# First transfers cut in smaller pieces, products of zeros ahead of the first data, and a new place for the tokens' turn, in a two-layer gated cross-attention kernel

## The reference

```python
x = x + tanh(g_xattn[0]) * xattn0(layernorm(x), ctx)   # 16 heads of 16, softmax over 361 rows, then 256-512-256
x = x + tanh(g_ffn[0])   * moe0(layernorm(x))          # best one of 8 experts, 256-1024-256
x = x + tanh(g_xattn[1]) * xattn1(layernorm(x), ctx)   # ternary weights, 8-bit activations, two attentions
x = x + tanh(g_ffn[1])   * moe1(layernorm(x))          # 16 mixed projections to q, k, v, attention, 16 back

# inside xattn0, the part that the change touches
q = (x @ Wq + bq)      # from the normalised tokens
k = (y @ Wk + bk)      # from the context, 8 x 361 x 256
v = (y @ Wv + bv)
```

## Time and profile before

| | us |
|---|---|
| median of 3 runs | 621.48 |
| lowest and highest of them | 619.89, 621.88 |
| the profiled execution, its own time | 621.23 |
| its span from first to last instruction | 619.4 |
| PE busy | 594.3 (96% of the span) |
| DVE, ACT, POOL busy | 322.6, 217.9, 72.4 |

### The profile page before, as it was taken

One profiled execution on the slowest core, in us unless ns is written; L12 is line 12 of the kernel. 1 busy time (PEld: TensorE's weight loads), 2 busy tenths in 40 slices (PEclk: granted clock), 3 DMA queues, 4 the chain that ended last, 5 costly groups with the idle time before them and its releaser, 6 DMA issues.

```text
span 619.4 us, 9464 instructions
## 1 busy us (share of the span) xinstructions
PE 594.3 (96%) x3699; PEld 397.3 (64%) x3699; DVE 322.6 (52%) x762; ACT 217.9 (35%) x509; POOL 72.4 (12%) x69
## 2 busy tenths in 40 slices
PE   5989999999999989999999889999999999999996
PEld 4756444444556758999999658777565555555653
DVE  3695767588774751222222789885562233231452
ACT  2644565645673364112221565673200010001000
POOL 0043101000004401232221000000100100000000
PEclk9999999989999978999999999999999999999999
DMA  8910000100001562899995100700723832320000
GB/s 195 318 68 2 17 2 1 35 3 2 2 1 26 194 206 72 304 341 344 361 341 206 62 2 0 239 2 3 261 77 103 313 103 77 103 76 1 0 26 26
DMA packets 25195, 69.93 MB, mean 113 GB/s; under 512 B 5143, under 2 KB 12919, under 8 KB 21319
## 3 DMA queue, kind: packets, MB, share of 16 engines
q1 hardware_dynamic: 21798, 58.16, 28.5%
q0 software_dynamic: 3360, 11.28, 5.3%
HBM read 64.62 MB, written 4.80 MB: 112 GB/s over the span
## 4 chain that ended last, share of the span: by engine, by line
PE 83%; DVE 8%; ACT 4%; DMA 2%; issue 1%; POOL 1%; SPq 0%; DVEq 0%; ACTq 0%; POOLq 0%
PE bank L2048 21%; PE bank L1565 12%; PE bank L1884 8%; PE bank L1897 8%; PE bank L1712 7%; PE bank L2084 7%; PE bank L1686 5%; PE bank L1730 3%; PE bank L1655 2%; ACT region L1459 2%; PE bank L1718 2%; DVE nmax L1007 1%; PE bank L1546 1%; DVE stage L1018 1%; PE bank L2002 1%
## 5 line engine op out<-in xcount | busy, mean ns | idle before, releaser
L2048 PE MATMUL bank<-region,kvT 128*128 128x400 f32 x384 | 130.4, 500 | 0.0
L2048 PEld LDWEIGHTS bank<-region,kvT 128*128 128x128 f32 x384 | 72.4, 190 | 54.2 <-issue 0.3
L1147 DVE TENSOR_TENSOR region<-xT,stage 128x800 f32<-128x800 f32 x30 | 29.7, 992 | 69.7 <-PE bank L2048 69.5
L718 DVE TENSOR_REDUCE nmax<-bank 100x2 f32<-100x722 f32 x64 | 55.2, 905 | 15.7 <-PE bank L1686 15.3
L1884 PEld LDWEIGHTS bank<-stage,region 128*128 128x128 f32 x448 | 52.2, 192 | 1.4 <-issue 0.8
L1884 PE MATMUL bank<-stage,region 128*128 128x128 f32 x448 | 52.4, 275 | 0.5 <-ACT stage L1394 0.5
L1897 PE MATMUL bank<-region,stage 128*128 128x256 f32 x224 | 50.7, 379 | 0.0
L1897 PEld LDWEIGHTS bank<-region,stage 128*128 128x128 f32 x224 | 41.5, 190 | 5.1
L2084 PE MATMUL bank<-region,kvt 128*128 128x400 f32 x128 | 43.9, 500 | 0.0
L919 DVE TENSOR_SCALAR stage<-bank,stage 128x128 f32<-128x128 f32 x56 | 15.8, 344 | 49.9 <-PE bank L1884 49.9
L1712 PE MATMUL bank<-xT,kvt 64*121 64x400 f32 (+1 forms) x144 | 39.5, 552 | 1.5 <-ACT kvT L1373 0.6
(11 more groups left out here) (343 smaller groups left out, 902.8 us busy)
## 6 DMA issues: line engine op xcount, KB each, us to landing
region<-in_e_w SPq DMA_DIRECT2D x28, 1024.0 KB, 5.2
kvT<-in_p_qkv SPq DMA_DIRECT2D x32, 384.0 KB, 3.1
stage<-w_dram POOLq DMA_DIRECT2D x2, 1600.0 KB, 12.7
stage<-in_t_f SPq DMA_DIRECT2D x1, 2048.0 KB, 15.0
kvt<-in_p_o SPq DMA_DIRECT2D x1, 2048.0 KB, 9.2
stage<-in_e_b SPq DMA_DIRECT2D x14, 128.0 KB, 5.9
region<-in_ctxT SPq DMA_DIRECT2D x3, 541.5 KB, 15.3
stage<-w_dram POOLq DMA_DIRECT2D x1, 1200.0 KB, 9.1
```

Source lines behind the costliest of these rows:

```text
L718: dve.tensor_reduce(nmax[:, b % 2, at_h:at_h + 9:8], banks[0:N, bank:bank + 2, 0:M], AX.X, ALU.max, negate=True)\
L1147: dve.tensor_tensor(x_w[n % NW], xT[:, :, at_h], w_bc[h][:, None, e, :].to_broadcast([P, 2, HT]), ALU.mult).then_inc(S["xw_done"], 1)
L2048: ins = pe.matmul(psum[3 * h + j][:, 0:HT], p_w[n % NP][:, k, j * HE:(j + 1) * HE], x_w[n % NW][:, k, :], start=e == 0 and k == 0, stop=e ...
```

## The change

Four edits, all in the first 30 us of the program.

1. The key and value weights load as two transfers of 192 KB. The key weights go first and signal context part 0's semaphore, which now counts to 32 (`CTX_LOADS`); the value weights follow context part 0 and signal `w_kv_in` with `cols`.
2. Context part 1 is issued ahead of `x` instead of behind it.
3. PE starts with six products of zeros (256 columns each, into bank 7) as soon as POOL has cleared `zero_tile`. Both operands read `zero_tile` with repeated elements. Then it runs `project_keys(0)` on `ctx_in0` alone, and waits for `w_kv_in` only ahead of `project_values(0)`.
4. `turn_tokens()` stands between the keys and the values of batch 3 instead of ahead of both. ACT's order is changed to match.

```diff
+CTX_LOADS = (2, 1, 1, 1, 1)
...
-            sp.dma_start(w_a[0:KC, 512:1536], d["w_a"][0:KC, 512:1536]).then_inc(S["w_kv_in"], 16)
+            sp.dma_start(w_a[0:KC, 512:1024], d["w_a"][0:KC, 512:1024]).then_inc(S["ctx_in0"], 16)
             load_context(0)
+            sp.dma_start(w_a[0:KC, 1024:1536], d["w_a"][0:KC, 1024:1536]).then_inc(S["w_kv_in"], 16)
             sp.dma_start(cols[:, 0:24], d["cols"]).then_inc(S["w_kv_in"], 16)
+            load_context(1)
             sp.dma_start(x[:, :, :], d["x"].rearrange("b n d -> n b d")).then_inc(S["x_in"], 16)
-            load_context(1)
...
-                dve.wait_ge(S[f"ctx_in{part}"], 16)
+                dve.wait_ge(S[f"ctx_in{part}"], 16 * CTX_LOADS[part])
...
             context_out(2)
+            context_keys_out(3)
             layernorm_turn()
-            context_out(3)
+            context_values_out(3)
...
-                pe.wait_ge(S[f"ctx_in{CTX_PART[b]}"], 16)
+                pe.wait_ge(S[f"ctx_in{CTX_PART[b]}"], 16 * CTX_LOADS[CTX_PART[b]])
...
+            pe.wait_ge(S["pool_step"], 1)
+            for _ in range(6):
+                pe.matmul(psum[7][:, 0:D], zero_tile[:, 0:1].to_broadcast([P, P]),
+                          zero_tile[:, None, :].to_broadcast([P, 4, D // 4]), start=True, stop=True)
+            project_keys(0)
             pe.wait_ge(S["w_kv_in"], 32)
-            project_context(0)
+            project_values(0)
             project_context(1)
             project_context(2)
+            project_keys(3)
             pe.wait_ge(S["consts_in"], 16)
             turn_tokens()
-            project_context(3)
+            project_values(3)
```

More of the change, by code:

```diff
@@ L1258, in half_turned, with context_keys_out @@
                     act.copy(xT[:, kk, h * HT:(h + 1) * HT], psum[4 + 2 * kk + h][:, 0:HT]).then_inc(S["xT_ready"], 1)
-            def context_out(b):
+            def context_keys_out(b):
                 for m in range(2):
@@ L1265, in context_out, with context_values_out @@
                                    bias=cols[:, 2 + m:3 + m]).then_inc(S["ctx_out"], 1)
+            def context_values_out(b):
                 if b == 0:
@@ L1272, in context_out @@
                         .then_inc(S["ctx_out"], 1)
+            def context_out(b):
+                context_keys_out(b)
+                context_values_out(b)
             act.wait_ge(S["w_kv_in"], 32)
```

## The result

| | before | changed |
|---|---|---|
| median of 5 runs, us | 620.78 | 617.40 |
| lowest to highest, us | 619.89 to 621.88 | 617.19 to 617.55 |
| ratio to before, 95% interval | | 0.9935 (0.9916 to 0.9954) |
| profiled execution, its own time, us | 621.23 | 617.29 |
| its span, us | 619.4 | 615.4 |

The kernel is faster by 0.65% (0.46 to 0.84 by the interval). The span is 4.0 us shorter, and only 2.80 of these have been won when the first score product starts. The other 1.2 come later, where the change touches nothing. The sum had 2.75 for the first part and nothing for the second.

A forecast was written before the change was run, and what follows sets the result against it. PE, busy for 96% of the span, was taken to bound the kernel. Batch 0 ending 2.9 us earlier, less 0.15 for transfers, gave 2.75 us off: 618.5 from the profiled 621.23, 618.7 from the median; forecast 618.6, range 617.0 to 621.2.

The forecast's parts named there:

- The sum: Whole kernel: batch 0 ends 2.9 us earlier, less 0.15 for split transfers, gives 2.75 us.
- From 43.2 on the chain is PE's again, and what follows waits on PE or on things that follow it: Behind the first score product: everything follows PE, so no further gain or loss was added.
- POOL follows on both of its sources: POOL's product before the first score: ACT's results 2.75 us earlier, DVE's passes 2.9, so the product shifts by 2.75.
- the likeliest case's own range: Whole kernel: 617.3 to 619.7 us if the forecast's mechanism, given 0.72, holds.
- Zeros and the clock: PE's start: zeros run 0.95 to 6.0, the clock rises at 6.45, batch 0 ends at 11.2, 2.9 us earlier.
- The rival in which zeros do not raise the clock: PE's start: keys still run at 1.2 GHz for 5.5 us, only 0.2 us gained, 621.0; chance 0.09.
- Context part 1 ahead of the tokens: Loads at the start: part 1 lands near 7.5, PE wants it at 11.2; cost nothing.
- Context part 2: Loads at the start: lands at 15.95, wanted at 16.2, 0.25 us in hand; late next, 0.15 us taken off.
- transfers take the gain: Loads at the start: part 2 lands at 17.2 to 17.9, PE waits, time 619.3 to 620.0; chance 0.14.
- The fixed cost of about 2.0 us of one DMA: Added transfer: if its fixed cost entered the stream, part 2 would land at 17.95, for a time of 620.1.
- The reason given for the turn's new place: Tokens' turn in batch 3: moving it behind the keys keeps out a wait of 0 to 0.5 us.
- The slower rival: POOL's product falls under DVE's long passes, ends at 44.8, PE idles 5.5 us, clock falls: 625.1; chance 0.05.

The follow-up runs named there:

- the later group: Ten runs of the changed kernel without any edit, beside the kernel before (621.19) on another chip: 619.32, ratio 0.997.
- the passes held back: Changed kernel with DVE's first long pass waiting for POOL's product: 622.35, ratio 1.003; also with early square root and five filling products at 213 to 217 us: 619.36, 0.995.

## Why the prediction was right or wrong

**The steps that failed.** Two steps of the prediction did. One is a term of the sum: "From 43.2 on the chain is PE's again, and what follows waits on PE or on things that follow it", which put at nothing what comes behind the first score. It measured 1.2 us in the profiled pair. The other is a mechanism: "POOL follows on both of its sources". The runs showed that POOL's product goes with DVE's passes, 21.93 us behind the reciprocal of the root, and not with PE; its number held all the same.

**The time.** 618.6 was forecast and 617.4 measured, inside the likeliest case's own range. The gain in spans was 4.0 where the sum had 2.75. The difference lies in the term put at nothing, and comes from the place and number of later clock falls. The prediction read two slow stretches off the trace before; there is a third, at 124 to 128 us, and 0.8 of the 1.2 us lie there. The term has no fixed size: the changed kernel had a rest of 575.0 in one trace and of 578.1 in another. The five runs of the result lie within 0.36 us of each other, and the ten of the later group reach from 616.29 to 621.62; the median of the fifteen is 618.73. So there are two measurements of what this change gives, 3.4 us (the result) and 1.9 (the later group, 621.19 less 619.32). The forecast of 2.75 us lies between them, and that is in part luck in how the falls lay.

**Zeros and the clock.** Right: zeros 0.92 to 6.2 (forecast 0.95 to 6.0), the clock up shortly behind 6.2 (6.45), batch 1 at 11.30 (11.2). The rival in which zeros do not raise the clock is excluded: eight key rows take 2.67 us with the zeros and 4.55 without.

**Context part 1 ahead of the tokens.** The step said "Cost nothing", which holds, but it did not say what the edit is worth. It carries the change. In the two traces without it PE waits 2.26 and 3.61 us and the clock falls a second time, and neither median shows a gain that is clear of the noise.

**Context part 2.** Right that it is late next, wrong that one number describes it. It was in at 15.7 in the first trace, with no wait. In six other traces with the new order PE waited 0.24 to 0.92 us for it, and in two 1.61 and 1.74, where the clock fell as well. The rival "transfers take the gain" is thus real as an event. The waits under 1 us are hidden as long as PE has its 1.17 us of slack behind them; the two long ones put the first score at 41.93 and 42.19. The fixed cost of about 2.0 us of one DMA that the prediction set against the cut (the Trainium skill, DMA: Bandwidth & Descriptors, section "Anatomy of one DMA — SWDGE (gpsimd) path") is given there for transfers that GpSimd issues, and these are issued by SP. The traces do not show such a cost added to the stream: with the added transfer part 2 landed at 15.7, 0.25 earlier than before, and joining the two transfers again did not bring it forward (a wait of 0.92). As landings vary by more than 1 us between executions, a cost of some tenths is not excluded. (In the prediction's working for that case 1.95 us should read 1.75, 17.95 less 16.2; its 620.1 is right.)

**The tokens and the root.** Tokens at 13.48 (13.8), root at 18.20 (18.1), turn at 23.76 (23.8): right. The reason given for the turn's new place, a wait of 0 to 0.5 us, was not confirmed.

**POOL's product.** The product ended at 40.37 for a forecast of 40.4, because the root moved by 2.8 and PE by 2.79, so both rules gave the same. The runs separate them. With PE 0.8 us later it stayed; with the root 1.75 us earlier, and PE only 0.34, it came 1.76 earlier. PE's gain counts only since ACT empties `context_out(1)` ahead of the root, and PE's own chain has 1.17 us of slack. The prediction had the 1.17 us in the earlier trace rows and read them as a gap that shifts along.

**The slower rival.** POOL did not slip to the end of both of DVE's passes. Its product is longer beside them (3.17 against 1.51 alone) and ends 1.39 us behind the first. The part of that rival on the clock holds: behind waits of 1.61, 1.74, 2.26 and 3.61 us during the loads PE ran at half speed, in all four traces that had one.

**What stays open.** Why POOL starts its product 1.6 us and more behind the last result it waits for even when DVE stands idle (36.92 to 38.50 with the passes held back; the profile's spans on POOL are rough), whether the fall at 121 to 124 hangs on the start, and what decides whether the clock falls at 354 and 429. None was tried.

## What to carry to other kernels

Idle time of the busiest engine right ahead of a product, as here 1.17 us, says that something else sets that moment: follow that chain back by itself (here POOL, DVE's passes, the root, a table load) before counting a gain of the busy engine. Warming PE up with idle products pays only if the data behind them keep coming; without the reordered loads it was a loss at the start in the trace (44.69 against 43.22). And a difference of 1 to 3 us in a kernel whose clock falls at changing places needs more runs, in more than one group, with a count of the slow stretches in each trace.

## What the runs showed of the hardware

- Products whose operands are zeros read with repeated elements bring PE to its full clock: 2.67 us for eight rows of 361 columns behind them, 4.55 without.
- At the start of the program the granted clock reads 1.00 although PE runs at half speed (the 4.55 us above against 2.59); after a wait of 2.26 us it reads 0.52 and then 0.50, and the durations agree (4.38).
- The same transfer, with the same bytes ahead of it, landed at different times in different executions: tokens at 13.48 and 14.34 in two traces of the same kernel, context part 2 without a wait and 0.45 us late.
- An elementwise product on POOL of 128 x 800 takes 1.51 us alone and 2.31 to 3.56 beside DVE's long passes, and it ended 1.34 to 1.35 us into the second of them, which is 1.37 to 1.39 behind the end of the first, whenever its record started (36.71 to 43.77).
